# Moving the first five weight chunks of a gated cross-attention layer from SyncE's DMA queue to ScalarE's

## The chip, the core and the metric

The kernel runs on one core of a Trainium2 chip. The metric is the device time of one execution in microseconds. A core has five engines that run their own programs and wait for each other on semaphores: TensorE (matrix products), VectorE, ScalarE, GpSimd and SyncE. Transfers between HBM and the on-chip memory (SBUF) are issued by SyncE, by ScalarE or by GpSimd, each into a queue of its own; sixteen transfer engines, common to all queues, move the data. In the profile SyncE's queue is q1, ScalarE's q10 and GpSimd's q0.

## The reference, cut to what matters

```python
# 8 batches x 128 tokens x 512; 32 heads of 128, 8 of k and v
q, k, v = layernorm(x) @ Wq, ctx @ Wk, ctx @ Wv
q, k = rope(q, pos), rope(k, pos)
attn = softmax(where(mask == 0, -1e9, q k^T / sqrt(128)))
x = x + tanh(g_xattn) * ((attn v) @ Wo)
x1, x2 = split(layernorm(x) @ w12^T + b12)
out = x + tanh(g_ffn) * ((silu(x1) * x2) @ w3^T + b3)
```

## The kernel before

Products in full precision are made of three in a reduced one: each factor is split in a high part (a copy by ScalarE that rounds) and a low part (value less high part, by VectorE or GpSimd), and TensorE adds high x high, low x high and high x low (`three`, L321). The main part is a loop over 8 groups of one k and v head and four q heads. Weights come in chunks of 256 KB (128 columns of Wk, Wv or Wq, or 128 rows of Wo) through a ring of five buffers, `raw`; ScalarE makes the high part of each chunk and GpSimd the low part (`split_chunk`, L673 and L913), and SyncE loads the next chunk into a buffer when both have read it (`load_chunk`, L272). The first chunks of group 0 are Wk, Wv and four of Wq. A chunk of Wk, Wv or Wq is read as four pieces of 512 bytes per partition, a batch of ctx or x (256 KB too) as one row of 2 KB per partition.

Ahead of the loop stands a prologue, and the change is there. Each engine's order in it is written out by hand:

- SyncE (L249 on) issues all first loads without a wait: ctx 0 and 1, chunk 0, ctx 2 and 3, chunk 1, x 0 to 3, chunks 2 to 4, ctx 4 to 7, x 4 to 7, the mask. Then chunk 5 waits for the splits of chunk 0 (L274, L275).
- ScalarE (L651 on) issues pos, the two gates and the bias b12. It then waits for both gates (L661) and takes their tanh (L662). After that it copies the tiles that TensorE has transposed: ctx 0 and 1, chunk 0, ctx 2 and 3, chunks 1 to 4, two rope tiles, then normalises x 2 and 3, copies v, the x tiles, v's high part, ctx 4 and 5, k's high part, chunk 5 (L757) and the rest.
- TensorE (L386 on) transposes ctx 0 to 3 as they land, projects k (`first_block(0)`), transposes the rope rows, projects v, transposes the normalised x 0 to 3, and goes on with v, ctx 4 to 7 and the q heads. Its first scores (L521) end the prologue.
- VectorE (L1026 on) corrects the positions, which GpSimd's gathers of rope rows need. Then come the low parts of ctx 0 to 3 (L1034), the statistics of x 0 to 3 (L1037, L1039), eleven tiny steps for 1/sqrt(var + eps) (`inv_std`, L1042: L1052 to L1057, Newton's method) and the shift (L1060), x 0 and 1 normalised (L1111), the rotation of k and the low parts of x 0 to 3; further on the same for the second half.
- GpSimd (L956 on) gathers the rope rows of 0 to 3, then makes the low parts of chunks 0 to 4 (L911) and adds the rotated parts of k.

Of the kernel before, what the change touches and what calls it, by code (L numbers as in the profile page):

```python
# [29 lines left out]
KT = E // 128  # L30
# [14 lines left out]
RAW = 5  # L45
# [17 lines left out]
def build(nc, x, ctx, pos, mask, g_x, g_f, Wq, Wk, Wv, Wo, w12, b12, w3, b3, out):  # L63
# [6 lines left out]
    def place(name, shape, dt, offset=None):  # L70

        size = int(np.prod(shape[1:])) * 4
        if offset is None:
            offset = at["top"]
            at["top"] += (size + 31) // 32 * 32
        at[name] = offset
        return nc.alloc_sbuf_tensor_at(name, shape, dt, offset=offset)

    def sem(name):
        return es.enter_context(nc.semaphore(name))  # L80

    with es:
# [8 lines left out]
        raw = place("raw", [128, RAW, 512], F32)  # L91
# [15 lines left out]
        ctx_raw = place("ctx_raw", [128, B, E], F32, at["q32"])  # L107
# [40 lines left out]
        ctx_loaded = [sem(f"ctx_loaded{i}") for i in range(B)]  # L148
        rope_loaded = [sem(f"rope_loaded{i}") for i in range(B)]
        raw_loaded = [sem(f"raw_loaded{i}") for i in range(RAW)]  # L150
# [31 lines left out]
        def chunk_src(kind, group):  # L182
            if kind == 0 or kind == 1:
                w = Wk if kind == 0 else Wv
                return w[:, bass.ds(group * D, D)].rearrange("(t p) c -> p t c", p=128)
            return Wq[:, bass.ds(group * (GH * D) + (kind - 2) * D, D)].rearrange("(t p) c -> p t c", p=128)

        def wo_src(group, h):
            return Wo[bass.ds(group * (GH * D) + h * D, D), :]
# [50 lines left out]
        def ffn_tile_src(t):  # L240

            if t < RAW:
                return raw[:, t, :], raw_loaded[t], 16 * ((W_FIRST + W_GROUP * KVH - 6 + t) // RAW + 1)
            if t < RAW + 4:
                return ffn_raw[:, t - RAW, :], ffn_loaded[t - RAW], 16
            return ffn_raw2[:, t - RAW - 4, :], ffn_loaded[t - RAW], 16


        @block.sync  # L249
        def _(sp):  # L250
            def rows(dst, src, b, s):
                sp.dma_start(dst[:, b, :], src[b]).then_inc(s[b], 16)

            def first_chunk(s):
                sp.dma_start(raw[:, s, :].rearrange("p (t c) -> p t c", t=KT), chunk_src(s, 0)).then_inc(raw_loaded[s], 16)
            for b in range(2):
                rows(ctx_raw, ctx, b, ctx_loaded)
            first_chunk(0)
            for b in range(2, 4):
                rows(ctx_raw, ctx, b, ctx_loaded)  # L260
            first_chunk(1)
            for b in range(4):
                rows(resid, x, b, x_loaded)
            for s in range(2, RAW):
                first_chunk(s)
            for b in range(4, 8):
                rows(ctx_raw, ctx, b, ctx_loaded)
            for b in range(4, 8):
                rows(resid, x, b, x_loaded)
            sp.dma_start(mask_raw[:, :, :], mask.rearrange("b q k -> q b k")).then_inc(mask_loaded, 16)  # L270

            def load_chunk(s, slot, src, parts):  # L272

                sp.wait_ge(act_whi, s - RAW + 1)  # L274
                sp.wait_ge(pool_wlo, s - RAW + 1)  # L275
                dst = raw[:, slot, :]
                if parts:
                    dst = dst.rearrange("p (t c) -> p t c", t=KT)
                sp.dma_start(dst, src).then_inc(raw_loaded[slot], 16)

            load_chunk(5, 0, chunk_src(5, 0), True)

            def group_loads(G, last):
                s0 = W_FIRST + W_GROUP * G
                for h in range(GH):
                    load_chunk(s0 + h, (W_FIRST + h) % RAW, wo_src(G, h), False)
                if not last:
                    for k in range(6):
                        load_chunk(s0 + 4 + k, (W_FIRST + 4 + k) % RAW, chunk_src(k, G + 1), True)

            with sp.Fori(0, KVH - 1) as G:
                group_loads(G, False)
            group_loads(KVH - 1, True)


            for t in range(FFN_TILES):
                dst, s, _ = ffn_tile_src(t)
                if t < RAW:
                    sp.wait_ge(act_whi, W_FIRST + W_GROUP * KVH - 6 + t - RAW + 1)
                    sp.wait_ge(pool_wlo, W_FIRST + W_GROUP * KVH - 6 + t - RAW + 1)  # L300
                elif t == RAW:
                    sp.wait_ge(pe_block, BLOCKS - 4)
                elif t == RAW + 4:
                    sp.wait_ge(act_qhi, 4 * (UNITS - 1))
                    sp.wait_ge(dve_qlo, 2 * (UNITS - 1))
                    sp.wait_ge(pool_qlo, 2 * (UNITS - 1))
                src = w12[t * 128:(t + 1) * 128, :] if t < 8 else w3[(t - 8) * 128:(t - 7) * 128, :]
                sp.dma_start(dst, src).then_inc(s, 16)
            sp.wait_ge(act_khi, UNITS)
            sp.wait_ge(pool_klo, UNITS)  # L310
            sp.dma_start(b3_row[:, :], b3.partition_broadcast(128)).then_inc(bias3_loaded, 16)

            for b in range(B):
                sp.wait_ge(dve_out, b + 1)
                sp.dma_start(out[b], resid[:, b, :]).then_inc(out_stored, 16)
            sp.wait_ge(out_stored, 16 * B)
# [334 lines left out]
        @block.scalar  # L651
        def _(act):
            act.dma_start(pos_raw[:, :], pos.rearrange("b s -> s b"), allow_slow_non_contiguous=True).then_inc(pos_loaded, 16)
            act.dma_start(graw[:, 0:1], g_x.partition_broadcast(128)).then_inc(gate_loaded, 16)
            act.dma_start(graw[:, 1:2], g_f.partition_broadcast(128)).then_inc(gate_loaded, 16)
            act.dma_start(b12_col[:, :], b12.rearrange("(t p) -> p t", p=128), allow_slow_non_contiguous=True).then_inc(bias_loaded, 16)
# [676 lines left out]
```

## Time and profile before

| | |
|---|---|
| median of 3 runs | 700.46 us (698.74, 700.46, 700.66) |
| span of the profiled execution | 698.7 us, 11562 instructions |
| busy: TensorE, VectorE, GpSimd, ScalarE | 97%, 76%, 51%, 47% of the span |
| chain that ended last: TensorE, VectorE, issue | 89%, 5%, 2% |
| SyncE's queue q1, ScalarE's q10, over the span | 31.20 MB, 0.01 MB |
| HBM read, written | 30.16 MB, 2.10 MB |

The profile gives the span, from the first to the last instruction; no time beyond it is shown for that execution, and the lowest of the three runs is equal to it within 0.1 us. The chain that ended last is followed back from the last instruction, at each step to what released it. In a row of the timeline, the brackets hold the engine's idle time before the instruction and what ended it. A load is shown by its issue on its queue, and apart from that by the time from issue to landing.

### The profile page before, as it was taken

The page shows a single profiled execution, that of the slowest core. Times are in us where ns is not written, and L with a number is a line of the kernel's source. Part 1 is how long each engine was busy: PE and PEld are TensorE (multiplying, and loading weights), DVE is VectorE, ACT ScalarE, POOL GpSimd, SP SyncE. Part 2 cuts the span into 40 slices and gives each one's busy share as a digit, 9 for nine tenths or more (in the row PEclk, how much of TensorE's full clock was granted, in tenths as well). Part 3 has the DMA queues.
Part 4 walks back from the last instruction along what each step waited for, and adds up shares of the span by engine and source line. Part 5 has one row for each costly group of instructions (what it writes and reads, how often), then busy time and mean ns, then how long its engine had stood idle before and what let it go on. Part 6 is the DMA issues. An engine that isn't in the chain of part 4 may idle for free.

```text
span 698.7 us, 11562 instructions
## 1 busy us (share of the span) xinstructions
PE 674.9 (97%) x3392; PEld 563.0 (81%) x3392; DVE 534.2 (76%) x878; ACT 330.9 (47%) x917; POOL 355.3 (51%) x298
## 2 busy tenths in 40 slices
PE   5878999999999999999999999999999999989998
PEld 4667888888888888888888888888888888868886
DVE  4987878787878788787878787878787878985433
ACT  3536453455345534553445445443545354875310
POOL 4534864486439544754475546653666446632000
PEclk9988999999999999999999999999999999999999
DMA  9700320031003100201021101210031005000002
GB/s 260 229 8 1 94 59 0 1 90 46 14 0 90 30 30 0 84 21 45 0 60 45 45 0 45 60 45 0 15 90 45 0 0 181 2 1 0 1 31 90
DMA packets 39090, 32.49 MB, mean 47 GB/s; under 512 B 4384, under 2 KB 29984, under 8 KB 39072
## 3 DMA queue, kind: packets, MB, share of 16 engines
q1 hardware_dynamic: 36320, 31.20, 14.9%
q0 software_dynamic: 384, 1.05, 0.5%
q10 hardware_dynamic: 2368, 0.01, 0.2%
q8 instruction: 10, 0.16, 0.1%
q14 instruction: 8, 0.07, 0.0%
HBM read 30.16 MB, written 2.10 MB: 46 GB/s over the span
## 4 chain that ended last, share of the span: by engine, by line
PE 89%; DVE 5%; issue 2%; ACT 1%; POOL 1%; DMA 1%; ACTq 0%; POOLq 0%; DVEq 0%
PE f_bank L323 12%; PE f_bank L325 11%; PE f_bank L324 11%; PE o_bank L323 9%; PE o_bank L325 9%; PE o_bank L324 9%; PE s_banks L433 6%; PE t_bank L329 4%; PE pv_bank L323 3%; PE pv_bank L325 3%; PE pv_bank L324 3%; PE s_banks L434 2%; PE pv_bank L329 1%; PE s_banks L325 1%; PE s_banks L323 1%
## 5 line engine op out<-in xcount | busy, mean ns | idle before, releaser
L686 ACT ACTIVATE prob<-prob,small 128x128 f32<-128x128 f32 x256 | 99.7, 391 | 132.1 <-DVE small L1148 132.1
L323 PE MATMUL o_bank<-wo_hi,o_hi 128*128 128x512 f32 x256 | 105.8, 413 | 0.0
L935 POOL TENSOR_TENSOR q<-t_cos,t_sin 128x512 f32<-128x512 f32 x64 | 82.4, 1289 | 45.8 <-DVE t_sin L1094 45.7
L323 PE MATMUL f_bank<-xT_hi,wq_hi 128*128 128x512 f32 x256 | 103.4, 404 | 0.9 <-ACT cT_hi L659 0.6
L325 PE MATMUL o_bank<-wo_hi,o_lo 128*128 128x512 f32 x256 | 100.4, 392 | 0.0
L325 PE MATMUL f_bank<-xT_hi,wq_lo 128*128 128x512 f32 x256 | 100.2, 391 | 0.0
L324 PE MATMUL f_bank<-xT_lo,wq_hi 128*128 128x512 f32 x256 | 100.0, 391 | 0.0
L324 PE MATMUL o_bank<-wo_lo,o_hi 128*128 128x512 f32 x256 | 100.0, 391 | 0.0
L950 POOL TENSOR_TENSOR prob<-prob,small 128x512 f32<-128x512 f32 x64 | 66.6, 1041 | 65.6 <-DVE small L1152 65.6
L659 ACT ACTIVATE o_hi<-pv_bank 128x512 fp32r<-128x512 f32 x64 | 38.2, 597 | 108.9 <-PE pv_bank L325 108.5
L1094 DVE TENSOR_TENSOR t_sin<-f_bank,rope 64x512 f32<-64x512 f32 x128 | 88.2, 689 | 1.8
L1143 DVE TENSOR_TENSOR prob<-s_banks,mfill 128x512 f32<-128x512 f32 x64 | 43.9, 686 | 37.3 <-PE s_banks L434 37.3
L911 POOL TENSOR_TENSOR q_lo<-q,q_hi 128x512 fp32r<-128x512 f32 x32 | 43.7, 1367 | 47.2 <-ACT q_hi L659 47.2
L433 PE MATMUL s_banks<-k_parts,q_hi 128*128 128x256 f32 x256 | 63.3, 325 | 3.8 <-issue 3.8
L1034 DVE TENSOR_TENSOR o_lo<-pv_bank,o_hi 128x512 fp32r<-128x512 f32 x64 | 44.1, 689 | 29.6 <-ACT o_hi L659 29.3
L935 POOL TENSOR_TENSOR k<-t_cos,t_sin 128x512 f32<-128x512 f32 x16 | 20.5, 1282 | 79.3 <-DVE t_sin L1093 79.3
L1164 DVE SCALAR_TENSOR_TENSOR resid<-o_bank,small,resid 128x512 f32<-128x512 f32 x64 | 48.0, 751 | 13.2 <-PE o_bank L325 12.3
L434 PE MATMUL s_banks<-k_parts,q_lo 128*128 128x128 f32 x256 | 57.2, 224 | 0.0
L325 PEld LDWEIGHTS o_bank<-wo_hi,o_lo 128*128 128x128 f32 x256 | 48.0, 188 | 10.9
L325 PEld LDWEIGHTS f_bank<-xT_hi,wq_lo 128*128 128x128 f32 x256 | 48.2, 188 | 10.4
L323 PEld LDWEIGHTS f_bank<-xT_hi,wq_hi 128*128 128x128 f32 x256 | 48.3, 189 | 9.9 <-ACT cT_hi L659 0.8
L324 PEld LDWEIGHTS f_bank<-xT_lo,wq_hi 128*128 128x128 f32 x256 | 48.4, 189 | 8.4
(162 smaller groups left out, 1559.3 us busy)
## 6 DMA issues: line engine op xcount, KB each, us to landing
raw<-in_L_xattn_Wq_dram SPq DMA_DIRECT2D x32, 256.0 KB, 2.9
raw<-in_L_xattn_Wo_dram SPq DMA_DIRECT2D x32, 256.0 KB, 2.6
ctx_raw<-in_ctx_dram SPq DMA_DIRECT2D x8, 256.0 KB, 7.0
raw<-in_L_xattn_Wk_dram SPq DMA_DIRECT2D x8, 256.0 KB
raw<-in_L_xattn_Wv_dram SPq DMA_DIRECT2D x8, 256.0 KB
resid<-in_x_dram SPq DMA_DIRECT2D x8, 256.0 KB, 7.0
out_dram<-resid SPq DMA_DIRECT2D x8, 256.0 KB, 2.0
ffn_raw<-in_L_ffn_w_dram SPq DMA_DIRECT2D x7, 256.0 KB, 5.0
```

Source lines behind the costliest of these rows:

```text
L323: nc.tensor.matmul(dst, st[0], mv_[0], start=start, stop=False)
L324: nc.tensor.matmul(dst, st[0], mv_[1], start=False, stop=False)
L325: return nc.tensor.matmul(dst, st[1], mv_[0], start=False, stop=stop)
L433: nc.tensor.matmul(s_banks[:, 256 * h:256 * (h + 1)], q_hi[:, sl, h, :], k_parts[:, ks, b, :], start=True, stop=False)
L434: mm = nc.tensor.matmul(s_banks[:, 256 * h:256 * h + 128], q_lo[:, sl, h, :], k_parts[:, ks, b, 0:128], start=False, stop=True)
L686: e = nc.scalar.activation(prob[:, k, h, :], prob[:, k, h, :], ACT.Exp, bias=nmin[k][:, h:h + 1], scale=-1.0, accum_out=psum_row[k][:, h:h ...
L935: nc.gpsimd.tensor_tensor(dst, t_cos[:, ts, :], t_sin[:, ts, :], ALU.add).then_inc(pool_rope, 1)
L950: nc.gpsimd.tensor_tensor(prob[:, k], prob[:, k], rrow[k].unsqueeze(2).to_broadcast([128, GH, S]), ALU.mult).then_inc(pool_norm, 1)
L1034: nc.vector.tensor_tensor(dst, src, f32(hi_part), ALU.subtract).then_inc(s, 1)
L1094: return nc.vector.tensor_tensor(dst, a, b_, ALU.mult)
L1143: nc.vector.tensor_tensor(prob[:, k], s_parts[:, :, 1, :], mfill[:, b, :].unsqueeze(1).to_broadcast([128, GH, S]), ALU.add).then_inc(dve_m ...
L1164: nc.vector.scalar_tensor_tensor(out=resid[:, b, :], in0=o_bank[k][:, :], scalar=tg_x, in1=resid[:, b, :], op0=ALU.mult, op1=ALU.add).then ...
```

## The change

The loads of chunks 0 to 4 leave SyncE's program and are issued by ScalarE, behind pos and ahead of the two gates and b12. SyncE's program begins with ctx 0 to 3 and x 0 to 3, then ctx 4 to 7, x 4 to 7 and the mask as before. Sources, destinations, semaphores and all waits stay.

```diff
--- before.py
+++ after.py
@@ -251,18 +251,10 @@
             def rows(dst, src, b, s):
                 sp.dma_start(dst[:, b, :], src[b]).then_inc(s[b], 16)
 
-            def first_chunk(s):
-                sp.dma_start(raw[:, s, :].rearrange("p (t c) -> p t c", t=KT), chunk_src(s, 0)).then_inc(raw_loaded[s], 16)
-            for b in range(2):
+            for b in range(4):
                 rows(ctx_raw, ctx, b, ctx_loaded)
-            first_chunk(0)
-            for b in range(2, 4):
-                rows(ctx_raw, ctx, b, ctx_loaded)
-            first_chunk(1)
             for b in range(4):
                 rows(resid, x, b, x_loaded)
-            for s in range(2, RAW):
-                first_chunk(s)
             for b in range(4, 8):
                 rows(ctx_raw, ctx, b, ctx_loaded)
             for b in range(4, 8):
@@ -651,6 +643,8 @@
         @block.scalar
         def _(act):
             act.dma_start(pos_raw[:, :], pos.rearrange("b s -> s b"), allow_slow_non_contiguous=True).then_inc(pos_loaded, 16)
+            for s in range(RAW):
+                act.dma_start(raw[:, s, :].rearrange("p (t c) -> p t c", t=KT), chunk_src(s, 0)).then_inc(raw_loaded[s], 16)
             act.dma_start(graw[:, 0:1], g_x.partition_broadcast(128)).then_inc(gate_loaded, 16)
             act.dma_start(graw[:, 1:2], g_f.partition_broadcast(128)).then_inc(gate_loaded, 16)
             act.dma_start(b12_col[:, :], b12.rearrange("(t p) -> p t", p=128), allow_slow_non_contiguous=True).then_inc(bias_loaded, 16)
```

## Rows read from the trace of the kernel before

**Rows 1.** Busy time of each engine: stretch, us, busy (x instructions), clock, DMA, GB/s
```profile
core 0: us, PE busy (x) PEld busy (x) DVE busy (x) ACT busy (x) POOL busy (x), PEclk, DMA share, GB/s
0.00:48.00 48.00, 33.64 (x159) 26.66 (x160) 36.80 (x75) 19.77 (x35) 25.05 (x27) 0.98 0.60 181
48.00:630.00 582.00, 575.77 (x2937) 482.26 (x2937) 469.21 (x755) 293.36 (x856) 327.63 (x269) 0.99 0.13 37
```

**Rows 2.** Chain of waits, 0 to 48 us: start us, us, what
```profile
1.89 5.49 DMA small<-in_g_ffn_dram
...
7.40 0.20 ACT small L662
...
10.99 0.69 DVE cT_lo L1034
...
15.37 0.18 DVE small L1052
...
16.16 1.14 DVE small L1057
...
18.58 1.23 DVE small L1056
...
20.70 1.00 DVE xnorm L1111 x2
...
46.39 0.55 PE s_banks L433
```

**Rows 3.** Timeline, ScalarE and TensorE: start us, us, instruction
```profile
2.85 1.28 ACT L662 ACT_TABLE_LOAD   x1 [2.85 <-issue]
...
8.27 2.05 PE L329 MATMUL o_bank<-ident,ctx_raw 128*128 128x128 f32 x8 [1.94 <-DMA ctx_raw<-in_ctx_dram]
...
9.42 0.60 ACT L659 ACTIVATE cT_hi<-o_bank 128x512 fp32r<-128x512 f32 x1 [0.33 <-issue]
...
21.39 1.08 PE L329 MATMUL o_bank<-ident,xnorm 128*128 128x128 f32 x8 [1.44 <-DVE xnorm L1111]
```

**Rows 4.** Timeline, GpSimd's low parts of the chunks
```profile
10.01 1.28 POOL L911 TENSOR_TENSOR wk_lo<-raw,wk_hi 128x512 fp32r<-128x512 f32 x1
...
16.00 3.78 POOL L911 TENSOR_TENSOR wq_lo<-raw,wq_hi 128x512 fp32r<-128x512 f32 x3 [3.18 <-ACT wq_hi L659]
```

**Rows 5.** Single loads: issue (start us, us), and us to landing
```profile
pos_raw<-in_pos_BxS_dram ACTq DMA_DIRECT2D x1, 4.0 KB, 3.5
...
6.34 0.48 SPq L255 DMA_DIRECT2D raw<-in_L_xattn_Wq_dram  x1
...
raw<-in_L_xattn_Wq_dram SPq DMA_DIRECT2D x1, 256.0 KB, 8.9
...
7.42 2.82 SPq L255 DMA_DIRECT2D raw<-in_L_xattn_Wq_dram  x1
...
raw<-in_L_xattn_Wq_dram SPq DMA_DIRECT2D x1, 256.0 KB, 9.6
...
15.40 0.43 SPq L252 DMA_DIRECT2D resid<-in_x_dram  x1
...
resid<-in_x_dram SPq DMA_DIRECT2D x1, 256.0 KB, 7.1
...
15.88 0.43 SPq L270 DMA_DIRECT2D mask_raw<-in_mask_BxSxS_ik_dram  x1
...
mask_raw<-in_mask_BxSxS_ik_dram SPq DMA_DIRECT2D x1, 512.0 KB, 8.4
```

**Rows 6.** DMA queues, 5.0 to 5.4 us, then 6.8 to 7.4 us
```profile
q1 hardware_dynamic: 102, 0.05, 43.3%
q10 hardware_dynamic: 26, 0.00, 2.9%
...
q1 hardware_dynamic: 87, 0.16, 69.5%
q10 hardware_dynamic: 375, 0.00, 34.9%
```

## The prediction, made before the changed kernel ran

> **What bounds the kernel now.** I read first the busy times by stretch. From 48 to 630 us TensorE is busy for 575.77 of 582 us, so nothing there waits for the other engines or for loads [rows 1]. The 48 us before that are different: TensorE works for 33.64 us of them, with the transfer engines at 0.60 of their time [rows 1]. All that the diff touches lies in this first stretch, and no later load has a fixed time: each one waits for a buffer. So what counts is when the first scores start (46.39 us, [rows 2]); a shift of that moment is a shift of the end, one for one.
>
> Then the chain of waits from 0 to 48 us. It starts with a transfer of four bytes per partition: the gate g_ffn, issued at 1.89, lands 5.49 us later, and only then can ScalarE run its tanh at 7.40 [rows 2]. Everything ScalarE does afterwards stands behind that wait in its program (the reader will find `act.wait_ge(gate_loaded, 32)` at L661, ahead of every tile copy). VectorE's first real work, the low parts of ctx, needs those copies; it ends at 10.99 + 0.69 = 11.68 [rows 2], and from there VectorE carries the chain almost without a gap: statistics to 15.37, the Newton steps, normalise from 20.70 [rows 2], and so on until the scores. Two things on this way matter below. ScalarE's third copy waited 0.33 us for TensorE, whose transposes of ctx 2 had waited 1.94 us for their load [rows 3]; the fourth waited about as long behind it. And three successive ones of the eleven tiny Newton steps, of which the first and the last stand in the rows, took 1.14 to 1.23 us in place of 0.18 like the first step of all [rows 2]: they stand inside GpSimd's three back-to-back subtractions, 16.00 to 19.78 [rows 4], each step ending when one of those does. From 16.16 to 18.58 + 1.23 = 19.81 that is 3.65, less 3 x 0.18 = 3.1 us lost on the chain. GpSimd runs them there because chunks 2 to 4 had only just landed.
>
> **The change, part by part.**
>
> (1) Five 256 KB loads go into ScalarE's queue between pos and the gates. ScalarE issues them itself, about 0.45 us each (a chunk's issue took 0.48, [rows 5]), 2.3 us together; an issue can also block, as the fifth chunk did on SyncE for 2.82 us [rows 5]. ScalarE now has 3.3 us of idle time before the tanh, between the end of its table load (2.85 + 1.28 = 4.13, [rows 3]) and 7.40. Whether the issues cost anything depends on part (2): if the gates come late, the blocked issues and the table load lie beside that wait, and I count them at nothing. Without this cover they would cost up to 2.3 + 2.8 + 1.3 - 3.3 = 3.1 us.
>
> (2) The gates now follow 1.28 MB in the same queue. A queue's loads have been landing in its order here, so the gates land when the five chunks have gone through. This is the main term. The transfer engines are full in this stretch, so the moment depends on how much of SyncE's queue passes meanwhile. The trace shows two queues beside each other twice. At 5.0 to 5.4 us SyncE's queue moved 102 packets of 512 bytes while ScalarE's moved 26 of the gates' [rows 6]. A chunk is four pieces per partition row, so 102 pieces are 25.5 rows against 26 gate rows: turns row for row. At 6.8 to 7.4 it was 375 four-byte pieces of b12 (eight to a row, 47 rows) against 87 packets [rows 6], that is 4.3 pieces to one; neither stretch is piece for piece. So I take row for row. Then five chunks go past with five ctx or x loads beside them, and the two gates with two more; with ctx 0, which is ahead of all, eight SyncE loads are through when the gates land. That is exactly the set that was through when chunk 4 landed before: eight ctx and x loads, five chunks, gates. It landed at 7.42 + 9.6 = 17.0 us [rows 5]. b12 (1024 pieces) was also ahead then and is behind now, some 0.4 us. So the gates land near **16.6 us**, 9.2 later than 7.4.
> Bounds: below, the five chunks alone after pos (0.75 + 3.5 = 4.25, [rows 5]), each 0.89 us (chunk 2 landed at 6.34 + 8.9 = 15.24, chunk 4 1.78 later), give 8.7; above, the whole of SyncE's queue first, its mask included, 15.88 + 8.4 = 24.3 us [rows 5].
>
> (3) Given back, first piece: with everything landed, TensorE's four ctx tiles are done long before the tanh. Both waits of a third of a microsecond go: **-0.7 us**. In detail, from the tanh: the last low part of ctx would end at +3.6 instead of +4.3.
>
> (4) Given back, second piece: all chunks are there, so ScalarE splits chunks 0 to 4 by about +4.9 and GpSimd, at 1.28 each [rows 4], runs its five subtractions from +1.8, +3.4, +4.7, +6.0 and +7.25, ending at +8.5. (Its gathers, which before held the first one until 10.01, are long over.) VectorE's statistics take 4 x 0.92 (15.37 less 11.68 before), to +7.3; the Newton steps meet only the last subtraction and wait some 1.2 us instead of 3.1: **-2.0 us**. Its bounds are 0 and -3.1; I take the middle because the order of both engines is fixed in the program. TensorE's first two blocks need their time from +3.6 to +11.8, and the x tiles had waited 1.44 us for VectorE [rows 3], so TensorE is about in time for the earlier normalised tile (+11.1).
>
> (5) SyncE's queue loses five issues. ctx 2, 3 and x 0 to 3 land earlier; nobody waits for them any more, because the tanh is later. ctx 4 to 7 are used after the four x tiles, now still later: nothing. The sixth chunk waits at L274 for the first split, which is late by about 9 us; ScalarE takes it only at L757, behind the four x tiles and the first k part, which the chain reaches some 15 us after the split, so even 9.6 us to landing, the longest of a chunk, stay hidden. pos stays first on its queue and the gathers stay where they are. Nothing.
>
> **Sum**: 9.2 - 0.7 - 2.0 = **+6.5 us**. On the profiled execution's span, 698.7, this is 705.2. The median of the runs shown is 700.46, 1.8 above that span (the runs lie between 698.74 and 700.66), so I forecast 700.46 + 6.5 = **707.0 us**. A difference of 0.3% (2.1 us) is about what a measurement can tell here.
>
> **The rivals.**
> - *Piece for piece.* If the transfer engines give one 512-byte piece of a chunk for one 2 KB row of ctx, a chunk passes four SyncE loads, and five chunks outlast all sixteen. The gates land with the mask, at about 24: 16.9 - 2.7 = +14.2, **714.7 us**. The 102 against 26 packets speak against it; what speaks for it is that the gates might then have been short of pieces for another reason. 0.08.
> - *Turns of some sixteen pieces.* Each transfer engine holds 32 pieces of a chunk and 8 of a ctx load. With turns as long as that, a chunk takes two turns and lets two loads by; five chunks and the gates let by twelve in place of seven. Each load costs 0.69 us (x 7 landed at 15.40 + 7.1 = 22.5, eight loads behind chunk 4 at 17.0, [rows 5]), so the gates land at 16.6 + 3.4 = 20: +9.9, **710.4 us**. The 375 against 87 packets are between the two readings and leave this open. 0.14. The Trainium skill (DMA: Bandwidth & Descriptors, Queues, rings and completion order) states such a rule: an engine drains a whole packet, typically 9 to 17 descriptors, from one ring before it switches; no row here shows the length of a turn directly.
> - *ScalarE's queue goes first.* The chunks run at nearly their own pace and the gates land at 9 to 12: between -1.1 and +1.9, plus part of the uncovered issues of part (1): **701 us**, no difference that can be told. Against it: in both windows SyncE's queue kept moving. 0.12.
> - *The gates overtake (the other side).* The chain is shorter if four-byte transfers don't stay behind the big ones. g_ffn would be issued at 1.89 + 2.3 = 4.2. If it lands as fast as pos did (3.5 us), the tanh is at 7.7, and parts (3) and (4) remain: 0.3 - 2.7 = -2.4, **698.1 us**. It decides for faster if the landing takes less than 3.8 us; at the 5.49 us of before it is no change. Against it: loads of one queue landed in order of issue throughout, and ScalarE's table load would have to be done. 0.03.
> - That the change does nothing cannot be, since the gates stand behind the chunks in the queue's own order.
>
> **How the numbers follow.** Row for row 0.63, turns of sixteen 0.14, piece for piece 0.08, ScalarE's queue first 0.12, overtaking 0.03. The likeliest case's own range is gates at 14 to 19 us, with 2.7 given back (bounds 0.7 and 3.8): 703 to 711. The other cases stretch it to **702.5 to 713.5**, leaving out overtaking, part of the case with ScalarE first, and the far end of piece for piece. Faster: 0.03. Within 0.3%: the case of ScalarE first and a little of the likeliest, 0.12. Slower: 0.85.
>
> **What would show it.** Right: the tanh starts at 15 to 18 us, ended by a transfer of the gate; the first scores start at 52 to 54; the Newton steps show one long instruction instead of three; from there on the trace of 48 to 630 us is the same, shifted. Wrong: a tanh before 12 us (the queues don't share by rows, or the gates overtook), a tanh after 20 (longer turns), a wait for x or ctx on the chain (SyncE's queue starved), or a ScalarE whose last DMA issue or table load ends later than the gates land (part 1 uncovered).

## The result, and the profile after

The changed kernel takes **711.38 us** (median of 4 runs, 709.64 to 712.39) against 700.18 for the kernel before on the same chip: ratio 1.0165, 95% interval 1.0141 to 1.0189. The profiled execution has a span of 710.6 us, 11.9 more than before, and the run itself took 712.39. (In every execution on record the time lies 1.8 to 1.9 us above its span. So the 1.8 us that the forecast put between span and median holds, and it was chance that the lowest run of before equalled the span.) It is slower, as forecast, and the median lies in the range, but 4.4 us above the forecast of 707.0: +11.2 where +6.5 stood.

The chain of waits of the changed kernel, 0 to 60 us, against [rows 2] (start us, us, what; line numbers of the changed file are 6 or 8 lower than before):

```profile
10.05 11.46 DMA small<-in_g_ffn_dram
...
21.53 0.20 ACT small L656
...
23.74 1.30 DVE cT_lo L1028 x2
...
25.13 0.77 PE f_bank L315
...
35.38 2.48 DVE xT_lo L1028 x4
...
58.02 0.55 PE s_banks L425
```

The gate g_ffn is now issued at 10.05 and lands at 21.51. The tanh runs at 21.53 instead of 7.40, 14.1 us later; the first scores start at 58.02 instead of 46.39, 11.6 us later. So 2.5 us are given back in between. From the scores on nothing has changed beyond 0.3 us (698.7 less 46.39 is 652.3 us, 710.6 less 58.02 is 652.6): in the 582 us behind the prologue TensorE is as busy as in [rows 1] (stretch, us, then each engine's busy time):

```profile
0.00:59.00 59.00, 33.73 (x157) 26.67 (x157) 34.53 (x75) 18.52 (x34) 24.95 (x27) 0.99 0.50 147
59.00:641.00 582.00, 575.70 (x2937) 482.21 (x2936) 468.17 (x754) 293.26 (x856) 326.85 (x269) 0.99 0.13 37
```

The timeline of the same stretch, against [rows 3] and [rows 4]:

```profile
2.44 3.36 ACTq L647 DMA_DIRECT2D raw<-in_L_xattn_Wq_dram  x3
...
5.83 4.19 ACTq L648 DMA_DIRECT2D small<-in_g_xattn_dram  x1
...
10.05 1.14 ACTq L649 DMA_DIRECT2D small<-in_g_ffn_dram  x1
...
11.71 1.28 ACT L656 ACT_TABLE_LOAD   x1 [11.71 <-issue]
21.53 0.20 ACT L656 ACTIVATE small<-small 128x2 f32<-128x2 f32 x1 [8.54 <-DMA small<-in_g_ffn_dram]
...
24.59 1.68 ACT L653 ACTIVATE wq_hi<-raw 128x512 fp32r<-128x512 f32 x3
...
26.03 3.74 POOL L905 TENSOR_TENSOR wq_lo<-raw,wq_hi 128x512 fp32r<-128x512 f32 x3
...
28.72 1.08 DVE L1046 TENSOR_SCALAR small<-small 128x4 f32<-128x4 f32 x1
...
29.84 0.17 DVE L1047 TENSOR_SCALAR small<-small 128x4 int32<-128x4 int32 x1
...
31.89 1.00 DVE L1105 TENSOR_SCALAR xnorm<-resid,small 128x512 f32<-128x512 f32 x2
...
35.38 1.29 DVE L1028 TENSOR_TENSOR xT_lo<-o_bank,xT_hi 128x512 fp32r<-128x512 f32 x2 [0.48 <-ACT xT_hi L653]
```

Three things are to be seen. ScalarE's DMA issues block: three chunks take 3.36 us, and g_xattn alone 4.19; the table load starts only at 11.71. But it ends at 12.99, and the wait for the gate goes on for 8.54 us more, so the issues lie beside that wait. Then the splits: all three Wq chunks run without a wait (24.59, 1.68 us), GpSimd subtracts without one behind them, and of VectorE's tiny Newton steps one alone (1.08) stands inside a subtraction, the others take 0.16 or 0.17. At last the low parts of x wait 0.48 us for ScalarE: TensorE's two projections had become the longer way (25.13 to 34.2 in the chain), not VectorE's steps. They took 9.1 us where they had taken 8.2 before; the part on the prediction comes back to this.

And the queues, against [rows 6]; q1 is SyncE's, q10 ScalarE's, first 4.8 to 5.2 us, then 15 to 19, then 20 to 21, and last the whole stretch from 7 to 21 (packets, MB, share of the sixteen engines' time):

```profile
q10 hardware_dynamic: 253, 0.13, 111.6%
q1 hardware_dynamic: 3, 0.01, 3.9%
...
q1 hardware_dynamic: 623, 1.14, 80.2%
q10 hardware_dynamic: 620, 0.31, 27.8%
...
q1 hardware_dynamic: 474, 0.24, 93.6%
q10 hardware_dynamic: 468, 0.01, 32.3%
...
q1 hardware_dynamic: 2370, 3.48, 72.4%
q10 hardware_dynamic: 2365, 0.92, 25.7%
```

In the first window ScalarE's queue is almost alone. In the second, 2 KB rows of x on q1 stand against 512-byte pieces of chunks on q10: 623 packets against 620 (by the bytes a few packets of either queue are much smaller than that). In the third it is 512-byte pieces of the mask against the four-byte pieces of the gates and of b12 behind them: 474 against 468. In both windows, and over the whole stretch from 7 to 21 us (2370 against 2365), each queue is served one piece for one piece, whatever the sizes: from 15 to 19 us q1 moved 1.14 MB and q10 0.31. Before 7 us it is not so. At 4.8 to 5.2 us the transfer engines are full too, and ctx 2 and 3, issued before 2.6 us, have not landed (TensorE starts on ctx 2 at 6.89), yet q1 moves 3 packets to q10's 253. What sets the shares in those first microseconds, no run shows.

### The profile page after: what moved, and what is told of

It is laid out like the page before. It is cut to its first block, busy times and chain, and to the rows that moved or that the text cites. A ratio compares the mean times of both kernels' runs of the same rounds, so it can differ in the third digit from the quotient of the medians.

```text
span 710.6 us, 11562 instructions
## 1 busy us (share of the span) xinstructions
PE 675.8 (95%) x3392; PEld 563.6 (79%) x3392; DVE 531.7 (75%) x878; ACT 330.2 (46%) x917; POOL 355.3 (50%) x298
## 4 chain that ended last, share of the span: by engine, by line
PE 89%; DVE 3%; issue 2%; DMA 2%; ACT 1%; ACTq 1%; POOL 1%; POOLq 0%; DVEq 0%
PE f_bank L315 12%; PE f_bank L317 12%; PE f_bank L316 12%; PE o_bank L315 9%; PE o_bank L317 9%; PE o_bank L316 9%; PE s_banks L425 6%; PE t_bank L321 4%; PE pv_bank L315 3%; PE pv_bank L317 3%; PE pv_bank L316 3%; PE s_banks L426 2%; DMA small<-in_g_ffn_dram 2%; PE pv_bank L321 1%; PE s_banks L317 1%
```

## The experiments

Each ratio compares executions that were run together; spans are of the profiled execution. The kernel before took 699.62 us (13 runs) beside the first four and 699.68 (35 runs) beside the other four.

| run | tanh starts | span | median | ratio, 95% interval |
|---|---|---|---|---|
| before | 7.40 | 698.7 | 700.18 | |
| changed | 21.53 | 710.6 | 711.38 | 1.0165 (1.0141 to 1.0189) |
| e1_gates_first | 13.05 | 704.5 | 706.09 | 1.0085 (1.0055 to 1.0115) |
| e2_small_pieces | 16.77 | 703.7 | 706.66 | 1.0100 (1.0072 to 1.0129) |
| e3_sync_holds | 15.92 | 704.0 | 705.76 | 1.0081 (1.0051 to 1.0110) |
| e6_two_chunks | 12.00 | 700.5 | 702.01 | 1.0025 (1.0009 to 1.0041) |
| e7_bias_last | 11.72 | 702.2 | 702.02 | 1.0033 (1.0017 to 1.0048) |
| e5_before_tanh_late | moved | 697.9 | 700.06 | 1.0008 (0.9993 to 1.0022) |
| e8_ctx_first | moved | 699.4 | 698.39 | 0.9981 (0.9969 to 0.9992) |
| e9_rope_earlier | moved | 697.1 | 699.15 | 0.9992 (0.9978 to 1.0006) |

**e2_small_pieces: is it pieces or rows?** This is the run that decides on the step that failed. The bytes, the number of loads and their places in the queues are those of the changed kernel; only the pieces of SyncE's ctx and x loads are a quarter as long.

```diff
-            for b in range(4):
-                rows(ctx_raw, ctx, b, ctx_loaded)
-            for b in range(4):
-                rows(resid, x, b, x_loaded)
+            def quarters(dst, src, g, s):
+                for q in range(4):
+                    w, bs = slice(q * 128, (q + 1) * 128), slice(4 * g, 4 * g + 4)
+                    sp.dma_start(dst[:, bs, w], src[bs, :, w].rearrange("b p c -> p b c")).then_inc(s[4 * g + q], 16)
+            quarters(ctx_raw, ctx, 0, ctx_loaded)
+            quarters(resid, x, 0, x_loaded)
...
-                    pe.wait_ge(ctx_loaded[b], 16)
+                    for q in range(4 if b % 4 == 0 else 0):
+                        pe.wait_ge(ctx_loaded[b + q], 16)
```

> The changed kernel, with SyncE's sixteen ctx and x loads of the same 256 KB each cut in 512-byte pieces (a quarter of the columns of four batches) instead of 2 KB rows. Theory A (one piece for one piece): a chunk now passes one SyncE load in place of four, so the gates land at 15 to 18 us instead of 21.5, though every SyncE load is itself slower; the span falls to about 705 to 707. Theory R (row for row, my forecast's reading) and theory T (turns of some fixed number of bytes): a row of the chunk already passed the same bytes as a ctx row, so the gates stay at 21 us or come later, since small pieces are slower to move; span 710 or more.

The gate in its chain, and its tanh in the timeline:

```profile
7.18 9.56 DMA small<-in_g_ffn_dram
...
16.77 0.20 ACT L657 ACTIVATE small<-small 128x2 f32<-128x2 f32 x1 [7.33 <-DMA small<-in_g_ffn_dram]
```

and its queues from 10 to 14 us:

```profile
q10 hardware_dynamic: 826, 0.41, 41.1%
q1 hardware_dynamic: 822, 0.41, 40.6%
q0 software_dynamic: 144, 0.39, 32.9%
```

The gates land at 16.75, inside 15 to 18, and 4.8 us ahead of the changed kernel's: g_ffn is issued 2.9 us earlier, since ScalarE's issues block for less long, and takes 9.56 us instead of 11.46. 826 packets against 822, and now 0.41 MB against 0.41: by equal counts the queues share bytes equally only when their pieces are equally long. (GpSimd's gathers, q0, moved 144 packets beside them, so equal counts are shown for the queues of SyncE and ScalarE alone.) Row for row is out, since it could not have moved the gates. The span of 703.7 is 1.3 below the range expected. Of the 6.9 us that it is below the changed kernel's, 5.2 are there at the first scores (52.85 against 58.02); the other 1.7 lie behind them, where this execution's granted clock was higher (0.86 from 50 to 62 us, against 0.72 from 55 to 67 in the changed kernel). Whether the edit has a part in that, the rows don't show.

**e3_sync_holds: who competes?**

```diff
+            sp.wait_ge(gate_loaded, 32)
             for b in range(4, 8):
                 rows(ctx_raw, ctx, b, ctx_loaded)
```

> The changed kernel, with SyncE waiting for both gates before it issues ctx 4 to 7, x 4 to 7 and the mask. Theory A: the chunks pass only SyncE's first eight loads and then move alone, so the gates land at 14 to 16.5 us, and the span falls to 703.5 to 706. The late ctx 4 to 7 are used 13 us after the tanh and cost nothing. Rival: the gates are late because ScalarE's own issues block (the issue of g_xattn took 4.19 us, and g_ffn was issued at 10.05 only); then holding SyncE back changes the landing by under 2 us and the span stays at 709 or above.

```profile
8.95 0.46 ACTq L650 DMA_DIRECT2D small<-in_g_ffn_dram  x1
...
15.92 0.20 ACT L657 ACTIVATE small<-small 128x2 f32<-128x2 f32 x1 [4.72 <-DMA small<-in_g_ffn_dram]
```

The tanh (15.92) and the span (704.0) are as theory A has them. With SyncE's second half held back, 5.6 us of the 14.1 go, though ScalarE's issues blocked here too (g_ffn was issued at 8.95, and landed 6.95 us later). So these 5.6 us are what SyncE's second half moves meanwhile; the other 8.5 are the five chunks, SyncE's first half beside them and the gates. The second half landing later cost nothing that shows: the scores start at 52.00, 36.1 us after the tanh, against 36.5 in the changed kernel.

**e6_two_chunks: the dose.** Only chunks 0 and 1 are ahead of the gates.

```diff
-            for s in range(RAW):
+            for s in range(2):
                 act.dma_start(raw[:, s, :].rearrange("p (t c) -> p t c", t=KT), chunk_src(s, 0)).then_inc(raw_loaded[s], 16)
```

(SyncE issues chunks 2 to 4 behind x 3, as before.)

> A dose between the two kernels: only chunks 0 and 1 go ahead of the gates on ScalarE's queue, chunks 2 to 4 stay on SyncE's, behind x 3 as before. Theory A (one piece for one piece, each chunk ahead of the gates lets about four SyncE loads by): the gates land at 11 to 13 us; with 0.7 and part of the Newton stall given back the span is 700.5 to 702.5. Row for row would put the gates at 8.5 to 9.5 and the span at 698 to 700. A cost in proportion to the number of chunks (11.9 us for five) would give 703.5.

```profile
12.00 0.20 ACT L658 ACTIVATE small<-small 128x2 f32<-128x2 f32 x1 [6.22 <-DMA small<-in_g_ffn_dram]
...
19.20 1.09 DVE L1048 TENSOR_SCALAR small<-small 128x4 f32<-128x4 f32 x1
```

Gates at 12.0, one Newton step held up, span 700.5, at the very edge of theory A's 700.5 to 702.5, and the median 2.4 above the kernel before. The gates decide: theory A had 11 to 13 us, row for row 8.5 to 9.5. The span alone, 0.5 above row for row's range, would not, and a cost in proportion to the chunks (703.5) is off by 3. For two chunks the start moves by 4.6 us, for five by 14.1.

**e1_gates_first: is it only the gates?** The four lines of the chunks' loop stand behind b12's issue instead of ahead of the gates'.

```diff
-            for s in range(RAW):
-                act.dma_start(raw[:, s, :].rearrange("p (t c) -> p t c", t=KT), chunk_src(s, 0)).then_inc(raw_loaded[s], 16)
             act.dma_start(graw[:, 0:1], g_x.partition_broadcast(128)).then_inc(gate_loaded, 16)
...
             act.dma_start(b12_col[:, :], b12.rearrange("(t p) -> p t", p=128), allow_slow_non_contiguous=True).then_inc(bias_loaded, 16)
+            for s in range(RAW):
+                act.dma_start(raw[:, s, :].rearrange("p (t c) -> p t c", t=KT), chunk_src(s, 0)).then_inc(raw_loaded[s], 16)
```

> The changed kernel with one thing moved: on ScalarE's queue the five chunks stand behind the gates and b12 instead of ahead of them. Theory A (the queues are served one piece for one piece, and the whole loss is the tanh's wait for gates behind five chunks): the tanh starts at 6 to 8 us again instead of 21.5. The chunks stay as late as in the changed kernel (chunk 4 at about 21.5 us), so ScalarE, which splits them ahead of the rope copies, starts its x normalisations some 2 us later than the kernel before: span 700 to 702, and 9 us under the changed kernel. Theory B (the five loads on a second queue cost by contention, wherever the gates stand): the span stays above 706.

```profile
4.22 7.51 ACTq L650 DMA_DIRECT2D raw<-in_L_xattn_Wq_dram  x3
...
11.75 1.28 ACT L656 ACT_TABLE_LOAD   x1 [11.75 <-issue]
13.05 0.20 ACT L656 ACTIVATE small<-small 128x2 f32<-128x2 f32 x1
...
15.41 0.63 ACT L653 ACTIVATE wk_hi<-raw 128x512 fp32r<-128x512 f32 x1 [1.19 <-DMA raw<-in_L_xattn_Wk_dram]
...
24.90 0.63 ACT L653 ACTIVATE wq_hi<-raw 128x512 fp32r<-128x512 f32 x1 [1.15 <-DMA raw<-in_L_xattn_Wq_dram]
```

The head of its chain:

```profile
2.85 12.54 DMA raw<-in_L_xattn_Wk_dram
```

Both theories missed. The span of 704.5 lies between them: with the gates ahead, 6.1 of the 11.9 us go. The tanh started at 13.05 and not at 6 to 8, and no gate was the cause: it came right behind ScalarE's table load, which came behind 7.51 us of three chunk issues. That is part (1) of the prediction with its cover gone. And chunk 0, which ScalarE needs third, landed at 15.4 us, where in the kernel before it never held ScalarE up; it, and not the tanh, heads the chain. Chunk 4 came at 24.9. So the chunks on this queue cost twice: what stands behind them waits, and they themselves come late.

**e7_bias_last: what did b12 weigh?** e1 with b12's issue behind the chunks' loop.

```diff
-            act.dma_start(b12_col[:, :], b12.rearrange("(t p) -> p t", p=128), allow_slow_non_contiguous=True).then_inc(bias_loaded, 16)
             for s in range(RAW):
                 act.dma_start(raw[:, s, :].rearrange("p (t c) -> p t c", t=KT), chunk_src(s, 0)).then_inc(raw_loaded[s], 16)
+            act.dma_start(b12_col[:, :], b12.rearrange("(t p) -> p t", p=128), allow_slow_non_contiguous=True).then_inc(bias_loaded, 16)
```

> e1_gates_first with one thing moved: b12, whose 4 KB are 1024 pieces of four bytes, stands behind the five chunks and not ahead of them (order on ScalarE's queue: pos, the two gates, chunks 0 to 4, b12). Theory A (one piece for one piece, whatever its size): 4 KB in 1024 pieces let as much of SyncE's queue by as two chunks do, so without them ahead chunk 0, which landed at 15.4 us in e1, lands before 10 us, and chunk 1 before 15. The tanh itself stays at 12 to 13.5 us, held by ScalarE's blocked issues and its table load. Span 700 to 702, from 704.5. Rival (bytes count, 4 KB are nothing): chunk 0 still lands after 14 us and the span stays within 1 us of 704.5.

Its timeline, the landing of chunk 0 (issued at 2.36), and a piece of its chain:

```profile
10.42 1.28 ACT L656 ACT_TABLE_LOAD   x1 [10.42 <-issue]
11.72 0.20 ACT L656 ACTIVATE small<-small 128x2 f32<-128x2 f32 x1
...
23.10 0.63 ACT L653 ACTIVATE wq_hi<-raw 128x512 fp32r<-128x512 f32 x1 [1.21 <-DMA raw<-in_L_xattn_Wq_dram]
```

```profile
raw<-in_L_xattn_Wk_dram ACTq DMA_DIRECT2D x1, 256.0 KB, 7.2
```

```profile
5.36 17.71 DMA raw<-in_L_xattn_Wq_dram
```

Chunk 0 lands at 2.36 + 7.2 = 9.6 us instead of 15.4. 4 KB of bias, as 1024 pieces of four bytes, had held it up for 5.8 us (0.5 of them by the issue of b12 alone, behind which the chunk was issued at 2.85). The span is 702.2, 0.2 above the range expected; the median, 702.02, is 2.3 above the kernel before. What is left is chunk 4: it lands at 23.07, where it had landed at 17.0 before [rows 5], and the chain rests on it. The tanh behind the blocked issues (11.72) is late as well, but not on this chain; what it would cost alone is not shown.

**e5_before_tanh_late: what was the gates' wait worth in the kernel before?**

```diff
-            act.wait_ge(gate_loaded, 32)
-            nc.scalar.activation(small[:, 24:26], graw, ACT.Tanh).then_inc(act_small, 1)
...
             tile_copy("rope", 3)
+            act.wait_ge(gate_loaded, 32)
+            nc.scalar.activation(small[:, 24:26], graw, ACT.Tanh).then_inc(act_small, 1)
```

> The kernel before, with the wait for the gates and the tanh moved down in ScalarE's program, behind the second rope tiles, where ScalarE waits anyway. It takes the gates off the head of the chain. Theory A: in the kernel before, that wait of 3.3 us is worth almost nothing, since the third and fourth ctx tiles wait for ctx 2 and 3, which land as late; the last low part of ctx still ends at 11.4 to 11.7 us, and the span stays within 0.7 us of 698.7. Rival: the chain is headed by the gates, as the profile of before has it, and the start moves up by the 2.7 us that ScalarE could begin earlier: span 696 to 697.

```profile
7.52 0.63 ACT L659 ACTIVATE wk_hi<-raw 128x512 fp32r<-128x512 f32 x1 [0.52 <-DMA raw<-in_L_xattn_Wk_dram]
...
8.60 2.12 PE L329 MATMUL o_bank<-ident,ctx_raw 128*128 128x128 f32 x8 [2.24 <-DMA ctx_raw<-in_ctx_dram]
...
11.38 0.69 DVE L1034 TENSOR_TENSOR cT_lo<-o_bank,cT_hi 128x512 fp32r<-128x512 f32 x1 [0.31 <-ACT cT_hi L659]
```

Nothing: ratio 1.0008, interval 0.9993 to 1.0022. ScalarE begins at 4.71 now and waits again at once: for chunk 0, then for the tiles of ctx 2, whose load TensorE awaits for 2.24 us. The last low part of ctx ends at 11.38 + 0.69 = 12.1, even 0.4 later than with the gates in front (I had 11.4 to 11.7). The gates headed the chain of the kernel before without bounding it; the loads of chunk 0, ctx 2 and ctx 3 were as late.

**e8_ctx_first and e9_rope_earlier: better orders.** Both keep all 256 KB loads in SyncE's queue and have the tanh late.

```diff
-            for b in range(2):
-                rows(ctx_raw, ctx, b, ctx_loaded)
-            first_chunk(0)
-            for b in range(2, 4):
-                rows(ctx_raw, ctx, b, ctx_loaded)
-            first_chunk(1)
+            for b in range(4):
+                rows(ctx_raw, ctx, b, ctx_loaded)
+            first_chunk(0)
             for b in range(4):
                 rows(resid, x, b, x_loaded)
-            for s in range(2, RAW):
+            for s in range(1, RAW):
                 first_chunk(s)
```

> e5, and SyncE's queue begins with ctx 0 to 3, then chunk 0, x 0 to 3, chunks 1 to 4; nothing but pos, gates and b12 on ScalarE's queue. All loads of 256 KB in one queue, so none is diluted. Theory A: the last low part of ctx ends at 9 to 10 us instead of 11.7; then chunk 4, which ScalarE splits ahead of the rope copies and which lands at 17 us as before, holds the rotation; net 1 to 3 us less than the kernel before: span 696 to 698. Rival: chunk 4 holds everything, no gain, span 698.5 to 699.

A wait in its timeline, then its chain:

```profile
8.96 0.63 ACT L656 ACTIVATE wk_hi<-raw 128x512 fp32r<-128x512 f32 x1 [2.23 <-DMA raw<-in_L_xattn_Wk_dram]
```

```profile
15.08 0.79 DVE small L1049
...
15.90 1.22 DVE small L1050
...
17.14 1.22 DVE small L1052
...
18.39 1.23 DVE small L1053
```

e8's ratio is 0.9981, interval 0.9969 to 0.9992: 0.2% below the kernel before, and by less than the 0.3% that I called measurable. Its profiled span (699.4) is above the expected 696 to 698 and shows no gain: ScalarE's order has chunk 0 ahead of ctx 2, so it waits 2.23 us for it, and the Newton steps, 0.3 us earlier, meet one more subtraction (four long steps, 15.08 to 19.62). The last low part of ctx ends at 11.39 and not at 9 to 10. The gain in the ratio goes with TensorE's mean granted clock, which is on record for each execution: it was 0.997 or 0.998 in 8 of e8's 12 runs and in 10 of the 35 of the kernel before. At 0.997 e8's seven runs took 697.64 to 698.54 us and the nine of the kernel before 697.73 to 698.35. At equal clocks the order of loads gains nothing; whether it has a part in the clock is not shown.

e9, against e8, has ScalarE copy ctx 2 and 3 ahead of chunk 0, and the rope tiles ahead of chunks 3 and 4:

```diff
-            first_chunk(0)
             tile_copy("ctx", 2)
             tile_copy("ctx", 3)
-            for s in range(1, 5):
+            for s in range(3):
                 first_chunk(s)
             tile_copy("rope", 0)
             tile_copy("rope", 1)
+            for s in range(3, 5):
+                first_chunk(s)
```

> e8, and ScalarE copies the rope tiles ahead of chunks 3 and 4. Theory A: the rope copies no longer wait for chunk 4 at 17 us, and first rotation and x tiles move up by another 1 to 2 us: span 695 to 697. Rival: the Newton steps inside GpSimd's subtractions take the place of that wait, span as e8 within 0.5 us.

```profile
44.64 0.55 PE s_banks L430
```

Its first scores start at 44.64, 1.75 us before the kernel before's, and its span is 697.1, 0.1 above theory A's range. By the ratio the twelve runs don't bear it out as a gain (0.9992, 0.9978 to 1.0006): they are spread over 697.3 to 700.4. But none of them had a clock above 0.995. At 0.994 e9's three runs took 697.74 to 697.95 us and the ten of the kernel before 699.09 to 700.09; at 0.992 the means are 699.8 (8 runs) and 700.7 (11). At equal clocks e9 is the faster one by 0.9 to 1.6 us, about what its first scores gain. This comparison was made after the fact, and whether e9's order itself brings the lower clocks is not shown.

## Why the prediction was right, and which step was off

The direction, the place and the wait were right: the tanh waits for gates that stand behind five chunks, the shift passes to the end, most of the given-back terms came. How the two queues share was wrong, and with it the size. That the median still lies in the range is partly luck: it is 0.4 us above the 703 to 711 of the case that I took for the likeliest, and inside only because the other cases had stretched the range. The tanh at 21.53 is one of the signs that the prediction named for being wrong ("a tanh after 20"), though not for the reason given there. By its own steps:

- *The main term* (part 2) is the one that failed: gates at 16.6 us by "row for row", measured 21.5. The term was +9.2 and is +14.1. Beside each other the queues give piece for piece (623 against 620 packets), the rival that I gave 0.08. e2, e3 and e6 each moved the gates into the range that this rule had set beforehand (15 to 18, 14 to 16.5 and 11 to 13 us; measured 16.75, 15.90 and 11.98).
- *Why I read it wrongly.* My evidence was 102 packets against 26 at 5.0 to 5.4 us [rows 6]. The same two rows say that the engines were busy for 43.3% and 2.9% of that window. They stood idle for half of it, so the counts cannot show how two queues share that both have work. The text named this objection and gave it too little weight. In the windows that decide, the shares add up to about 100% or more. Full engines are not enough, though: at 6.8 to 7.4 us [rows 6] and at 4.8 to 5.2 us of the changed kernel they were full and the counts far from equal (375 against 87, 253 against 3). Equal counts set in at about 7 us in the changed kernel and hold from there to the gates.
- *The rival's own price* was off too, 24 us against 21.5. It let all of SyncE's queue by. But around 5 us ScalarE's queue had the engines nearly for itself (253 packets against 3), so chunk 0 passed much less than four loads. Had I taken 21.5, that rival's sum would have been 14.1 - 2.7 = +11.4 us; measured +11.9 in the span and +11.2 in the median.
- *Turns of some sixteen pieces*: as I put this rival, a chunk lets two loads by, so its queue would move two pieces to SyncE's one, with the gates at 20. The landing at 21.5 is too near to exclude that; the counts of 15 to 19 us do. The Trainium skill (DMA: Bandwidth & Descriptors, Queues, rings and completion order) has an engine drain a packet of some 9 to 17 descriptors before it switches. The counts here fit turns of any length that are equal for both queues and not cut off at the end of a load; how long a turn is, no run shows.
- *Part (1)*, issues at nothing because covered: right in the changed kernel, where 8.54 us of wait were left over. The price without cover was bounded at 3.1 us. That sum counts the table load twice: the 3.3 us of idle time begin behind it, so it should have been 2.3 + 2.8 - 3.3 = 1.8. e1 shows the price larger than either: the issues end at 11.73, the tanh starts 5.65 us later than in [rows 2], with gates issued before 2.4 us.
- *Part (3)*, -0.7: the last low part of ctx ended 11.68 - 7.40 = 4.28 us after the tanh, and now 25.04 - 21.53 = 3.51. Measured -0.8.
- *Part (4)*, -2.0: from the first Newton step to the normalisation 5.33 us before (15.37 to 20.70), 3.17 now (28.72 to 31.89), -2.2. But 0.4 of the two was lost again: I had TensorE "about in time", done with its first two blocks 11.8 us after the tanh, and it was done after 12.7 (34.23), so that VectorE waited 0.48 us for the first x copy. In sum 2.5 instead of 2.7. TensorE's own pace made it late, as its chain shows:

```profile
29.74 0.43 PE f_bank L316
...
33.99 0.24 PE f_bank L317
```

  All twelve products of the first block follow each other at 0.43 us (the first at more), those of the second at 0.23; in the kernel before the pace changed at about 15 us, after eight products. TensorE had been idle for 16.0 us ahead of the block here and for 1.5 there. The profile gives the granted clock as 1.00 in both stretches, so what set the pace is not shown.
- *Part (5)*, nothing: right. No x, ctx or later chunk stands in the chain of the changed kernel.

## What to carry to other kernels

Loads on a second queue got no second share of the bandwidth here, they got turns, and a load cut in short pieces gave most of the bytes to a neighbour with long ones: before splitting loads over queues, compare the length of their pieces, not their sizes. A tiny load that a program waits for belongs ahead of everything on its queue, and an engine that computes should not be the one to issue many large loads, for its issues blocked it here for up to 7.5 us. And a ratio of two queues from a trace says nothing about sharing where the transfer engines stand idle half the time, and even with full engines a window of half a microsecond can mislead: take it over the whole stretch that the wait covers.

## What the hardware showed that I had not expected

- The equality of the counts, to about 1% (623 and 620; 474 and 468; 826 and 822; 2370 and 2365 over 14 us), for pieces of 2048, 512 and 4 bytes. The Trainium skill (DMA: Bandwidth & Descriptors, Issuing engines are not separate DMA queues) says that issuing from several engines saves only issue time; here even that was not saved, since the issues moved to an engine with other work, and the unequal sharing came on top.
- 4 KB of bias in 1024 pieces delayed the chunk behind it by 5.8 us (e1 against e7). How its four-byte pieces take turns is not settled: at 6.8 to 7.4 us in the kernel before there were 4.3 of them to one of SyncE's [rows 6], and in e1 at 7 to 8 us ScalarE's queue moved 593 packets to SyncE's 149.
- The issue of a single tiny load, g_xattn's, took 4.19 us behind the five chunks; on SyncE a chunk's had taken 2.82 [rows 5].
- TensorE's granted clock just after the first scores differs between executions of nearly the same program. The stretch 44 to 56 us of the kernel before, then of e5:

```profile
44.00:56.00 12.00, 9.53 (x44) 8.25 (x44) 8.83 (x16) 6.53 (x16) 3.71 (x4) 0.72 0.00 1
```

```profile
44.00:56.00 12.00, 8.35 (x44) 7.01 (x44) 10.05 (x21) 7.76 (x19) 4.47 (x4) 0.86 0.00 1
```

The clock is 0.72 in the mean there and 0.86 in e5, whose first scores come no earlier and whose span is 0.8 us shorter. TensorE had been idle for 3.7 to 3.8 us ahead of the scores in both. Runs of one kernel lie up to 4.7 us apart here (697.73 to 702.39 for the kernel before); their times go with the mean granted clock on record for each: of the 35 beside e5, the ten at 0.997 or 0.998 took 697.73 to 698.36 us, the eleven at 0.992 took 700.07 to 701.26, and the one at 0.988 took 702.39. e5's shorter span is of this kind: behind its first scores it took 651.0 us, the kernel before 652.3. What sends an execution one way or the other no run here shows.
